# Gate and up of a mixture-of-experts layer with the weights as the loaded operand and the token weight moved behind the down product

## The reference

```
probs = softmax(xn @ gate_w.T); top 4 of 16 experts per token, weights normalised
act   = silu(xn @ Wg) * (xn @ Wu)            # Wg, Wu: 512 x 384, one pair per expert
y_e   = act @ Wd                             # Wd: 384 x 512
out   = x + tanh(g) * (y_shared + sum over the 4 chosen experts of weight_e * y_e)
```

## Time and profile before

| | us |
|---|---|
| median of three runs | 735.83 |
| profiled execution | 733.4 |
| its span | 731.6 |
| preparation, routing logits, scales | 0 to about 103 |
| shared tiles 2 to 15 | about 103 to 212 |
| routed slots, from the first gate matmul to the end of the span | 214.4 to 731.6 |

### The profile page before, as it was taken

How to read it: one execution, slowest core, us unless ns; L and a number is a source line. 1 busy time by engine, 2 the same in 40 slices (tenths; PEclk the granted TensorE clock), 3 DMA queues, 4 the chain that set the end, 5 groups by cost and what they waited for, 6 DMA issues and landing times.

```text
span 731.6 us, 17952 instructions
## 1 busy us (share of the span) xinstructions
PE 631.8 (86%) x4586; PEld 387.6 (53%) x4587; DVE 525.2 (72%) x1299; ACT 316.9 (43%) x542; POOL 319.1 (44%) x504
## 2 busy tenths in 40 slices
PE   4112769999999699999999999999999999899992
PEld 3012445666656366556555565555555555565660
DVE  5999778877598586768887867688678888767210
ACT  2333573222234345455444454554444554445441
POOL 1464620000113454546456455554656455465532
PEclk9655769999999899999999999999999999999997
DMA  7661135110216679485866866767585776655432
GB/s 226 214 185 50 68 102 138 59 58 2 73 31 174 148 170 185 90 205 99 187 146 140 205 126 153 164 126 185 118 172 120 174 190 113 167 96 98 83 48 39
DMA packets 48524, 93.73 MB, mean 128 GB/s; under 512 B 7677, under 2 KB 15339, under 8 KB 48498
## 3 DMA queue, kind: packets, MB, share of 16 engines
q0 software_dynamic: 16128, 38.35, 29.6%
q1 hardware_dynamic: 32370, 55.07, 25.2%
HBM read 65.16 MB, written 28.24 MB: 128 GB/s over the span
## 4 chain that ended last, share of the span: by engine, by line
DMA 48%; PE 27%; DVE 10%; POOL 5%; issue 4%; ACT 2%; POOLq 2%; SPq 1%; DVEq 0%; ACTq 0%
DMA out<-mix_room,idx_s 46%; PE gu_ps L1113 15%; PE bank L1140 6%; DVE stats L671 2%; PE bank L1166 2%; POOL idx_s L480 2%; POOL pool_tick L458 2%; PE bank L1127 1%; DMA room_b<-token_rows,idx_g 1%; POOL mix_room L410 1%; POOLq L462 1%; DVE wgu L872 1%; PE bank L1152 1%; DMA out<-X 1%; ACT xT L532 1%
## 5 line engine op out<-in xcount | busy, mean ns | idle before, releaser
L1113 PE MATMUL gu_ps<-wgu,mix_room 128*128 x1728 | 305.4, 327 | 1.7 <-DVE tick L895 1.7
L1113 PEld LDWEIGHTS gu_ps<-wgu,mix_room 128*128 128x128 f16 x1728 | 166.4, 98 | 113.1 <-issue 8.0
L1140 PE MATMUL bank<-wdn,aT 128*128 (+1 forms) x792 | 186.1, 380 | 1.4 <-ACT aT L570 1.0
L570 ACT ACTIVATE aT<-bank 128x768 f16<-128x768 f16 x88 | 71.3, 810 | 144.1 <-PE bank L1127 137.1
L483 POOL DMA_INDIRECT out<-mix_room,idx_s x72 | 120.2, 1669 | 19.3 <-issue 19.1
L1140 PEld LDWEIGHTS bank<-wdn,aT 128*128 128x128 f16 x792 | 77.7, 98 | 86.6 <-issue 4.2
L939 DVE SCALAR_TENSOR_TENSOR act<-gu_ps,wslot,sg x72 | 44.5, 618 | 93.9 <-ACT sg L556 82.8
L467 POOL COPY idx_g<-room_b 128x1 int32 x72 | 56.1, 780 | 120.0 <-issue 100.1
L480 POOL COPY idx_s<-room_b 128x1 int32 x72 | 16.6, 230 | 192.1 <-DMA out<-mix_room,idx_s 164.3
L563 ACT ACTIVATE acth<-act 128x384 f16<-128x384 f32 x88 | 46.0, 523 | 120.6 <-DVE act L939 111.0
L470 POOL DMA_INDIRECT room_b<-token_rows,idx_g x72 | 78.1, 1084 | 11.2 <-issue 1.7
(11 more groups left out here) (156 smaller groups left out, 665.1 us busy)
## 6 DMA issues: line engine op xcount, KB each, us to landing
dn_sc<-dn_scale_halves SPq DMA_DIRECT2D x34, 384.0 KB
dn_raw<-in_L_ffn_down_packed SPq DMA_DIRECT2D x48, 256.0 KB
gu_sc<-gu_scale_halves SPq DMA_DIRECT2D x34, 192.0 KB
X<-in_x SPq DMA_DIRECT2D x4, 1024.0 KB, 11.6
token_rows<-room_a SPq DMA_DIRECT2D x16, 256.0 KB, 2.1
out<-X SPq DMA_DIRECT2D x4, 1024.0 KB, 4.5
gu_raw<-in_L_ffn_gate_up_packed SPq DMA_DIRECT2D x16, 192.0 KB
gu_raw<-in_L_ffn_gate_up_packed SPq DMA_DIRECT2D x16, 191.9 KB
```

The source lines that it names most:

```text
L570: nc.scalar.activation(aT[:, b].rearrange("p a c t -> p (a c t)"), at_ps, ACT.Copy).then_inc(aT_done, 1)
L1113: mm = nc.tensor.matmul(ps[b][:, 0:I], x(xp * HC + c), wgu[:, w, wp, c, col:col + I], start=(c == 0 and xp == 0 and wp == 0), stop=(c == H ...
L1140: mm = nc.tensor.matmul(y_ps[b][:, :], aT[:, b, ap, t, :], wdn[:, w, wp, t, :], start=(n == 0), stop=(n == 3 * IC - 1))
```

## The change

`gate_up` loads slices of 128 columns of `wgu` and moves the 128 tokens. One half of it is now all of gate, the other all of up: 3 column tiles of 384, 4 chunks, 3 parts, 36 matmuls of 128 columns each. g and u come out with the hidden features on the partitions and the tokens in the columns, which is the form that `down` loads, so `transpose_act`, `copy_aT` and the tile `acth` go, and `high_halves` and `low_halves` write straight to `aT`. Two semaphores (`g_done`, `u_done`) take the place of `gu_done`: Silu waits for gate only, `activations` for up as well. The token weight can no longer be a scalar per partition of the activation. It is applied in `take_y`, as the scale of the down result; `take_weight` reads one column of the gathered rows at a register's offset for it, at the beginning of ScalarE's slot, after the `take_y` of the slot before. In shared tiles `shared_w` moves to `add_y`.

```diff
@@ -200,7 +199,7 @@
         iota_s = sb("iota_s", [P, SLOTS], F32)
         idx_g = sb("idx_g", [P, 2], I32)
         idx_s = sb("idx_s", [P, 2], I32)
-        wslot = sb("wslot", [P, 2, E], F32)
+        wslot = sb("wslot", [P, 2], F32)
         xTs = xn.rearrange("p b h -> p (b h)").bitcast(F16).rearrange("p (b n) -> p b n", b=2)
         y_sb = xmix
...
@@ -545,12 +542,8 @@
             copy_xT(NT - 2)
             copy_xT(NT - 1)
-            def activate(s, b):
-                gate(s, b)
-                high_halves(s, b)
-
             def gate(s, b):
-                a.wait_ge(gu_done, s + 1)
+                a.wait_ge(g_done, s + 1)
                 if not isinstance(s, int) or s >= 2:
                     a.wait_ge(act_done, s - 1)
                 nc.scalar.activation(sg[:, b, :], g_ps[b][:, 0:I], ACT.Silu,
@@ -559,32 +552,29 @@
             def high_halves(s, b):
                 a.wait_ge(act_done, s + 1)
                 if not isinstance(s, int) or s >= 2:
-                    a.wait_ge(at_done, s - 1)
-                nc.scalar.activation(acth[:, b, 0, :], act[:, b, :], ACT.Copy).then_inc(ah_done, 1)
-
-            def copy_aT(s, b):
-
-                a.wait_ge(at_done, s + 1)
-                if not isinstance(s, int) or s >= 2:
                     a.wait_ge(y_done, s - 1)
-                nc.scalar.activation(aT[:, b].rearrange("p a c t -> p (a c t)"), at_ps, ACT.Copy).then_inc(aT_done, 1)
+                nc.scalar.activation(aT[:, b, 0].rearrange("p c t -> p (c t)"), act[:, b, :], ACT.Copy).then_inc(ah_done, 1)
             def take_rows(r, b):
-                a.wait_ge(xg_ld[b], 8 * (r - b) + 16)
-                if not isinstance(r, int) or r >= 2:
-                    a.wait_ge(act_done, NT + r - 1)
-                nc.scalar.activation(wslot[:, b, :], xg[:, b, H:ROW], ACT.Copy).then_inc(wslot_done, 1)
                 a.wait_ge(tx_done, r + 1)
                 if not isinstance(r, int) or r >= 2:
-                    a.wait_ge(gu_done, NT + r - 1)
+                    a.wait_ge(u_done, NT + r - 1)
                 nc.scalar.activation(xTs[:, b, :], xT_ps, ACT.Copy).then_inc(xTs_done, 1)
+
+            def take_weight(r, b):
+
+                e = a.value_load(slot_i[0:1, 0, bass.ds(r, 1)], min_val=0, max_val=E - 1)
+                if not isinstance(r, int) or r >= 2:
+                    a.wait_ge(yev_done, r - 1)
+                nc.scalar.activation(wslot[:, b:b + 1], xg[:, b, bass.ds(H + e, 1)], ACT.Copy).then_inc(wslot_done, 1)
             def take_y(r, b):
                 a.wait_ge(y_done, NT + r + 1)
+                a.wait_ge(wslot_done, r + 1)
                 if not isinstance(r, int) or r >= 2:
                     a.wait_ge(added, 16 * (r - 1))
-                nc.scalar.activation(y_sb[:, b, :], y_ps[b][:, :], ACT.Copy, scale=1.0 / W_SCALE).then_inc(yev_done, 1)
+                nc.scalar.activation(y_sb[:, b, :], y_ps[b][:, :], ACT.Copy, scale=wslot[:, b:b + 1]).then_inc(yev_done, 1)
             for i in range(2):
@@ -594,22 +584,22 @@
             a.wait_ge(lg_ps_ready, NT)
             nc.scalar.activation(lgh[:, :, :], lg_ps[:, :].rearrange("p (t k e) -> p t k e", k=2, e=E)[:, :, 1, :],
                                  ACT.Copy).then_inc(lgh_ready, 1)
-            copy_aT(0, 0)
             a.wait_ge(lsub_ready, 1)
             nc.scalar.activation(r_exp[:, :, :], lg[:, :, :], ACT.Exp).then_inc(exp_ready, 1)
             for i in range(2, NT):
-                copy_aT(i - 1, (i - 1) % 2)
+                gate(i, i % 2)
                 if i == NT - 1:
                     take_rows(0, 0)
-                activate(i, i % 2)
+                high_halves(i, i % 2)
             a.wait_ge(route_ready, 1)
             inner = a.value_load(pairs_i[0:1, 0:1], min_val=E // 2 - 2, max_val=SLOTS // 2 - 2)
             def slot(r, b, rows=True):
-                copy_aT(r + (NT - 1), 1 - b)
+                take_weight(r, b)
+                gate(NT + r, b)
                 if rows:
                     take_rows(r + 1, 1 - b)
-                activate(NT + r, b)
+                high_halves(NT + r, b)
                 if not isinstance(r, int) or r >= 1:
                     take_y(r - 1, 1 - b)
             for r in range(4):
...
@@ -704,7 +693,7 @@
                 nc.vector.tensor_tensor(xhl[:, i % ROWS_AHEAD, 1, :], xn[:, i % 2, :], xhl[:, i % ROWS_AHEAD, 0, :],
                                         ALU.subtract).then_inc(xl_ready, 1)
-            step(nc.vector.tensor_scalar(shared_w[:, :], tg[:, 1:2], 1.0 / (X_SCALE * W_SCALE), None, ALU.mult))
+            step(nc.vector.tensor_scalar(shared_w[:, :], tg[:, 1:2], 1.0 / W_SCALE, None, ALU.mult))
             def route():
@@ -931,21 +920,26 @@
             dequant(0, 0, None, PARTS - 1)
             end_dequant(0)
-            def activations(s, b, weight):
+            def activations(s, b):
                 if not isinstance(s, int) or s >= 2:
-                    v.wait_ge(at_done, s - 1)
+                    v.wait_ge(ah_done, s - 1)
+                    v.wait_ge(al_done, s - 1)
                 v.wait_ge(sg_done, s + 1)
-                nc.vector.scalar_tensor_tensor(act[:, b, :], gu_ps[:, 2 + b, 0:I], weight, sg[:, b, :], ALU.mult,
-                                               ALU.mult).then_inc(act_done, 1)
+                v.wait_ge(u_done, s + 1)
+                nc.vector.scalar_tensor_tensor(act[:, b, :], gu_ps[:, 2 + b, 0:I], 1.0 / (X_SCALE * W_SCALE), sg[:, b, :],
+                                               ALU.mult, ALU.mult).then_inc(act_done, 1)
             def low_halves(s, b):
                 v.wait_ge(ah_done, s + 1)
-                nc.vector.tensor_tensor(acth[:, b, 1, :], act[:, b, :], acth[:, b, 0, :], ALU.subtract).then_inc(al_done, 1)
+                if not isinstance(s, int) or s >= 2:
+                    v.wait_ge(y_done, s - 1)
+                nc.vector.tensor_tensor(aT[:, b, 1].rearrange("p c t -> p (c t)"), act[:, b, :],
+                                        aT[:, b, 0].rearrange("p c t -> p (c t)"), ALU.subtract).then_inc(al_done, 1)
             def add_y(i):
                 v.wait_ge(y_done, i + 1)
-                nc.vector.scalar_tensor_tensor(X[:, i, :], y_ps[i % 2][:, :], 1.0 / W_SCALE, X[:, i, :], ALU.mult,
+                nc.vector.scalar_tensor_tensor(X[:, i, :], y_ps[i % 2][:, :], shared_w[:, 0:1], X[:, i, :], ALU.mult,
                                                ALU.add).then_inc(acc_done, 1)
             def first_weights(k):
@@ -995,21 +989,19 @@
             for i in range(2):
-                activations(i, i, shared_w[:, 0:1])
+                activations(i, i)
             for i in range(2):
                 low_halves(i, i)
             route()
             add_y(0)
             for i in range(2, NT):
-                activations(i, i % 2, shared_w[:, 0:1])
+                activations(i, i % 2)
                 low_halves(i, i % 2)
                 add_y(i - 1)
                 after_shared_slot(i)
             def head(r, e):
-                b = r % 2
-                v.wait_ge(wslot_done, r + 1)
-                activations(r + NT, b, wslot[:, b, bass.ds(e, 1)])
+                activations(r + NT, r % 2)
             def routed_slot(r, e):
                 head(r, e)
@@ -1107,28 +1099,20 @@
                 if half == 0 and (not isinstance(s, int) or s >= 2):
                     pe.wait_ge(act_done, s - 1)
-                for c in range(half * HC // 2, (half + 1) * HC // 2):
-                    for xp, wp in ((0, 0), (0, 1), (1, 0)):
-                        for ps, col in ((g_ps, 0), (u_ps, I)):
-                            mm = nc.tensor.matmul(ps[b][:, 0:I], x(xp * HC + c), wgu[:, w, wp, c, col:col + I],
-                                                  start=(c == 0 and xp == 0 and wp == 0),
-                                                  stop=(c == HC - 1 and xp == 1), skip_group_check=True)
-                if half == 1:
-                    mm.then_inc(gu_done, 1)
-
-            def transpose_act(s, b):
+                ps, done = ((g_ps, g_done), (u_ps, u_done))[half]
+                for t in range(IC):
+                    col = half * I + t * P
+                    n = 0
+                    for c in range(HC):
+                        for wp, xp in ((0, 0), (0, 1), (1, 0)):
+                            mm = nc.tensor.matmul(ps[b][:, t * P:(t + 1) * P], wgu[:, w, wp, c, col:col + P], x(xp * HC + c),
+                                                  start=(n == 0), stop=(n == 3 * HC - 1))
+                            n += 1
+                mm.then_inc(done, 1)
+
+            def down(s, b, w):
                 pe.wait_ge(ah_done, s + 1)
                 pe.wait_ge(al_done, s + 1)
-                if not isinstance(s, int) or s >= 1:
-                    pe.wait_ge(aT_done, s)
-                for hl in range(2):
-                    for t in range(IC):
-                        k = hl * IC + t
```

(18 more changed lines are left out.)

## The result

The changed kernel took 934.15 us, median of four runs (932.12 to 939.08), against 735.34 for the kernel before on the same chip (four runs, 732.65 to 740.84): a ratio of 1.272, 95% interval 1.264 to 1.281. The forecast was 906, range 885 to 945, slower with a chance of 0.92. The profiled execution of the changed kernel took 939.08, its span 937.4; two further executions took 935.46 and 943.74.

The account below looks back on a forecast made before the run. PE's sequencer was taken to become the bound at 9.35 us per routed slot: first routed gate at 212.4, 71 slots in 663.9, then the end, span 902; plus 1.8 and 2.4 gives 906 us, range 885 to 945.

Parts of the forecast that it names:

- The bound: Routed slots: PE's sequencer, one step of 0.125 us per distinct weight slice, exceeds the array's 6.4 and the adds' 6.96 us.
- The count, 48: Routed gate_up: 48 distinct weight slices per slot instead of 16, adding 32 register steps, 4.0 us per slot.
- the 9.1 to 9.6 that the sum gave: Routed slot on the sequencer: 5.3 to 5.8, minus 0.2, plus 4.0 us; the middle, 9.35, was taken.
- The bound of 9.9: Routed slot: up to 9.9 us if a loaded operand's address costs more than a moving one's; 945 us in all.
- The span: Whole kernel: first routed gate at 212.4, 71 slots of 9.35 in 663.9, then the end, together 902 us.
- The correction for the profiled execution: From span to median time: 2.4 us added because the earlier profiled execution was 2.4 below its median, besides 1.8 outside the span.
- the 2 us taken: Start of the routed slots: 2 us earlier, between 0 and 3.5, from array and VectorE savings in shared tiles.
- the 2.8 of array time in the forecast: Shared tiles, with constant addresses: 14 tiles at 0.2 us less array time each, 2.8 us.
- The pace of the pairs: Array, gate_up: load and matmul pairs of 128 columns at 56 ns each, 72 in 4.03 us.
- ScalarE, POOL and the gather: Routed slots: ScalarE's work, POOL's adds and the gather waiting behind take_y all stay hidden in a 9.35 us slot.
- The rival in which the sequencer stays hidden: Routed slots: fewer register steps issued, array 6.4 us, 732 us total; late gather could add up to 14 x 3; chance 8%.
- The clock: Routed slots: rival that gaps in gate and up drop PE's clock to 1.2 GHz, about 970 us; chance 8%.

Follow-up runs that it names:

- experiment 1: Changed kernel, but in routed slots gate_up loads 48 fixed slices of xT instead of wgu slices (wrong numbers, no register addresses): 751.59 us, ratio 1.021.
- experiment 3: Changed kernel with 36 distinct weight slices per routed slot instead of 48, same 72 matmuls (part of the low products left out): 824.56 us, ratio 1.120.
- experiment 2: Kernel before, its gate_up cut into 72 matmuls of 128 moving weight columns, tokens still loaded, transposes kept: 932.68 us, ratio 1.267.
- experiment 8: Changed kernel with PE's register load for down moved ahead of the up half: 916.35 us, ratio 1.245.
- Experiment 10: Changed kernel with fixed xT slices for routed gate_up (wrong numbers), weights copied aside early and 80 do-nothing VectorE instructions: 729.57 us, ratio 0.996.
- experiments 5 and 9: Kernel before with only the token weight moved to take_y, plus 30 VectorE memsets: 750.52 us; the same with weights copied aside early: 731.35 us.
- experiment 4: Kernel before with only the token weight moved from the activation to take_y, gate and up untouched: 791.08 us, ratio 1.075.

## Why the prediction was right, step by step

**The bound.** The sequencer became the bound, for the reason given: experiment 1 takes 183 us away by leaving out these addresses, experiment 3 gives 0.127 us per address where 0.125 was read from the earlier trace rows, and experiment 2 rules out that an address of a loaded operand costs more or less than that of a moving one. The count, 48, is shown.

**The slot was sized too small**, 9.35 us against 9.81, which is above the 9.1 to 9.6 that the sum gave. Two terms were missing. The register load before `down` was priced at today's 0.30 us; it took up to 0.98 in that place, and moving it gave back 0.25 us per slot (experiment 8). And one step in six (574 of 3312) stands 129 to 340 ns behind the one before it instead of 124: 48 x (129.7 - 124) = 0.27 us. 9.81 - 0.25 - 0.27 = 9.29, beside the 9.35 assumed. What makes the load slow is open, and so is what makes the longer steps: the first distance in each half is long in 143 of 144, mostly about 180 ns, and after it mostly every eighth, at places that shift from slot to slot. The kernel before shows longer distances too, 78 of the 360 within `down`'s runs of steps, but there its sequencer also paused for other reasons that the trace does not tell apart. The bound of 9.9 held these terms by luck: it was written down for another reason, that an address of a loaded operand might cost more, and that was not so.

**The span.** Forecast: first routed gate at 212.4, 71 slots in 663.9, 25.7 behind slot 71's start, together 902. Measured: 214.21, 696.7, and 937.4 - 910.94 = 26.5: 1.8 + 32.8 + 0.8 = 35.4 us too little. The correction for the profiled execution went the wrong way besides: 2.4 us were added, and this one was 4.9 above the median, which is why the median is only 28 off. If the median execution began its routed slots as experiment 8 did, at 210.2, the start was 2.2 us too late in the forecast, and the terms close on the time: 906 - 2.2 + 32.8 + 0.8 - 2.4 = 935.0, beside 934.15.

**The start.** The profile hides a gain that was larger than the 2 us taken, and larger than its bound of 3.5. From the first shared gate and up to the first routed gate the kernel before took 214.36 - 78.31 = 136.05 us, the changed kernel 214.21 - 82.92 = 131.29, and experiment 8 210.18 - 78.12 = 132.06: 4.0 to 4.8 us less. The tiles from number 2 on give 2.5 of it, near the 2.8 of array time in the forecast (4.02 us a tile in place of 3.90 + 0.34); the rest lies between the first two tiles and tile 2, for which the forecast had no term. The array still waits for VectorE's tick at the end, 1.96 us for 1.75, but the tick comes earlier too.

**The pace of the pairs.** 56 ns was right over 8, 36 and 72 pairs. The Trainium skill, "TensorE: Matmul & The Clock Gate", section "Back-to-back issue gap", gives about 81 ns for such a stream; these runs differ from it where addresses are constant (56 ns), and the measurement decides. The 87 ns of the routed slots resemble it by chance: they are two register steps for three pairs, 2 x 129.7 / 3 = 86 ns, and experiment 3, with as many pairs and fewer steps, has them 66 ns apart.

**ScalarE, POOL and the gather.** In the changed kernel they were hidden, as forecast: POOL waits for the weight and no longer for the add. The rival in which the sequencer stays hidden was priced at 732 us and up to 14 x 3 more for the late gather. Experiment 1 is that case, and its 751.59 lies inside, but not by these terms alone. Experiment 10 shows the 732 (729.57), and experiments 5 and 9 put the late gather at some 16 us, inside its bound; what no term held is VectorE's fetching, 40.6 us in experiment 4. How the 22 us between experiments 1 and 10 divide between the two was not measured.

**The clock** stayed at 0.98 to 1.00 in the routed windows; that rival was wrong.

## What to carry to other kernels

Where a buffer is picked by a register, count the distinct slices addressed through it, loaded or moving, not the columns: here each cost 0.124 us of the sequencer, and cutting a 384-column operand in three tripled them, with an array that had 0.2 us less to do. A sequencer that is hidden shows itself in the median of its waits against a satisfied one; that difference, divided by the price of a step, is an estimate of the steps that may be added before the array waits (here 0.84 / 0.124, some 7; no run tests that number). And before a form is made faster on the array, look at who sets the pace: with every known obstacle removed it was worth at most 0.4%, because the adds were the next bound where weights load, and new holes of unknown cause stood before the array behind the last load. And compare two profiles from a point that the change cannot have moved: here 4.6 us lost in the preparation hid the whole gain of the shared tiles.

## What was not expected of the hardware

An engine can stop for its own instructions. In experiment 4 VectorE's loop of two experts stopped eight times in 398 us, 54.3 us in all, and the instruction queue moved 39 packets instead of 14; 30 memsets of one element ahead of the loop brought the packets back to 14 and the time from 791.08 to 750.52. That the place of the loop in memory decides is an inference from this; in the changed kernel 30 did not help (40 packets), and 80, in a program that also differed by the early copy, did (15).

A register load on PE's sequencer takes 0.30 us most of the time, and up to 1 us in some places of some programs: median 0.56 before `down` in the changed kernel, 0.30 every time in the same place of experiment 2 and after the move of experiment 8, median 0.46 at the beginning of the slot in experiment 3. Why was not found; a run of register steps ahead of it does not explain it. And with pairs 86 ns apart for 56 ns of work, the granted clock stayed at 0.98 to 1.00 over the windows shown.
